# Four transformer layers on one core: the rotation reads queries and keys from the projection's bank, and two orders are changed in the attention slots

## The reference

```python
q = (x @ Wq).reshape(B, S, H, hd).transpose(0, 2, 1, 3)   # 32 heads of 16
k = (x @ Wk).reshape(B, S, G, hd).transpose(0, 2, 1, 3)   # 8 groups
v = (x @ Wv).reshape(B, S, G, hd).transpose(0, 2, 1, 3)
q = _apply_rope(q, cos, sin)          # t * cos + rotated * sin
k = _apply_rope(k, cos, sin)
scores = jnp.einsum('bhqd,bhkd->bhqk', q, k)               # keys repeated 4 times
scores = jnp.where(causal[None, None], -jnp.inf, scores)
attn = jax.nn.softmax(scores / jnp.sqrt(jnp.float32(hd)), axis=-1)
ctx = jnp.einsum('bhqk,bhkd->bqhd', attn, v).reshape(B, S, D)
return ctx @ Wo
```

## Time and profile before

| | |
|---|---|
| median of 3 runs | 1228.06 us (1227.69 to 1230.71) |
| the profiled execution's own time | 1229.5 us |
| its span | 1227.8 us |
| busy: TensorE matmul | 1149.5 us (94%) |
| busy: VectorE | 782.8 us (64%) |
| busy: ScalarE | 655.9 us (53%) |
| busy: GpSimd | 506.8 us (41%) |
| mean granted TensorE clock | 0.989 |
| slots of run 0 end | about 545 us |
| slots of run 1 begin | about 835 us |

### The profile page before, as it was taken

How to read it: one execution, slowest core, us unless ns; L and a number is a source line. 1 busy time by engine, 2 the same in 40 slices (tenths; PEclk the granted TensorE clock), 3 DMA queues, 4 the chain that set the end, 5 groups by cost and what they waited for, 6 DMA issues and landing times.

```text
span 1227.8 us, 22076 instructions
## 1 busy us (share of the span) xinstructions
PE 1149.5 (94%) x8476; PEld 845.0 (69%) x8476; DVE 782.8 (64%) x1124; ACT 655.9 (53%) x1199; POOL 506.8 (41%) x648
## 2 busy tenths in 40 slices
PE   5999999999999999989999999999999999899997
PEld 4788877766656656556687788777666667676565
DVE  7843458786875646674644465545777887875545
ACT  4433348675565555554323333326866666766654
POOL 0000127565422112124555454512965566655552
PEclk9999989999999999999999999998999999999999
DMA  7000010030000100010242222211000100000001
GB/s 275 1 1 1 1 36 3 2 114 2 2 2 2 39 1 2 27 53 27 79 153 85 96 77 81 94 42 50 6 2 2 43 2 20 19 17 34 2 1 69
DMA packets 15258, 48.04 MB, mean 39 GB/s; under 512 B 2858, under 2 KB 6959, under 8 KB 14388
## 3 DMA queue, kind: packets, MB, share of 16 engines
q1 hardware_dynamic: 15156, 46.63, 11.3%
HBM read 44.00 MB, written 2.10 MB: 38 GB/s over the span
## 4 chain that ended last, share of the span: by engine, by line
PE 67%; DVE 18%; ACT 6%; issue 5%; DMA 2%; POOL 2%; DVEq 0%; ACTq 0%; SPq 0%; POOLq 0%
PE bank L679 18%; PE bank L812 13%; PE bank L712 9%; PE bank L950 8%; DVE negmax L1906 6%; PE bank L925 5%; PE bank L863 3%; PE bank L905 3%; ACT probs L1446 2%; DMA W_lo_whole<-in_w 2%; DVE rope_sin L1893 1%; PE bank L829 1%; DVE W_lo_whole L1676 1%; PE bank L872 1%; DVE pvT L1934 1%
## 5 line engine op out<-in xcount | busy, mean ns | idle before, releaser
L1906 DVE TENSOR_REDUCE negmax<-bank 128x4 f32<-128x1024 f32 (+1 forms) x256 | 250.0, 1016 | 75.7 <-PE bank L872 56.6
L1446 ACT ACTIVATE probs<-bank 128x512 f32<-128x512 f32 (+1 forms) x224 | 188.2, 846 | 48.0 <-PE bank L905 46.8
L2139 POOL TENSOR_SCALAR_AFFINE_SELECT probs<-probs 128x512 f32<-128x512 f32 x192 | 128.3, 678 | 136.7 <-ACT probs L1446 135.8
L2061 POOL TENSOR_TENSOR W_lo<-W_lo_whole,W_hi 128x512 fp32r<-128x512 f32 x84 | 117.2, 1424 | 100.6 <-ACT W_hi L1175 100.6
L925 PE MATMUL bank<-probs,V 128*32 128x256 f32 (+1 forms) x2048 | 117.7, 348 | 6.7 <-DVE negmax L1906 3.5
L863 PE MATMUL bank<-kT,qT 64*128 64x256 f32 (+1 forms) x1024 | 102.1, 295 | 10.5 <-DVE xT_lo L1557 5.5
L1175 ACT ACTIVATE W_hi<-W_lo_whole 128x1536 fp32r<-128x1536 f32 x28 | 41.7, 1489 | 131.4 <-DVE W_lo_whole L1676 131.4
L1457 ACT ACTIVATE pv<-bank 128x256 f32<-128x256 f32 x128 | 49.7, 388 | 109.2 <-PE bank L925 97.4
L905 PE MATMUL bank<-qT,kT 64*128 64x256 f32 (+1 forms) x512 | 97.4, 396 | 11.0 <-ACT qT L1418 3.3
L2108 POOL TENSOR_TENSOR scaled<-pvT,recip 128x256 f32<-128x256 f32 x64 | 41.9, 654 | 146.5 <-DVE recip L1937 146.2
L925 PEld LDWEIGHTS bank<-probs,V 128*32 128x32 f32 x2048 | 54.0, 110 | 62.2 <-issue 28.9
(11 more groups left out here) (214 smaller groups left out, 2687.2 us busy)
## 6 DMA issues: line engine op xcount, KB each, us to landing
W_lo_whole<-in_w SPq DMA_DIRECT2D x28, 768.0 KB, 4.2
Wqkv_lo_whole<-in_Wqkv SPq DMA_DIRECT2D x6, 768.0 KB, 7.0
Wo_lo_whole<-in_Wo SPq DMA_DIRECT2D x4, 1024.0 KB, 4.9
Wqkv<-in_Wqkv SPq DMA_DIRECT2D x2, 1536.0 KB, 7.2
Wdown_whole<-in_Wd SPq DMA_DIRECT2D x1, 2816.0 KB, 14.8
x<-in_x SPq DMA_DIRECT2D x4, 512.0 KB, 6.2
out<-x SPq DMA_DIRECT2D x8, 256.0 KB, 2.0
V_lo_whole<-in_V SPq DMA_DIRECT2D x1, 1408.0 KB, 6.1
```

What stands on the lines that cost most here:

```text
L1446: nc.scalar.activation(A[l].probs[gi % 2][kb][:, :, q0 - kb * A[l].probs1:].rearrange("p (b h) q -> p b h q", b=2), B.tensor(key)[:, :, 0: ...
L1906: v.tensor_reduce(A[l].negmax[u % 2][:, qb, :].rearrange("p (b h) -> p b h", b=2)[:, :, 2 * g:2 * g + 2], B.tensor(key)[:, :, 0:2 * nk].re ...
L2061: ins = gp.tensor_tensor(lo, whole, hi.bitcast(F32), ALU.subtract)
L2139: gp.affine_select(out=blk, in_=blk, compare_op=ALU.is_ge, fill=0.0, base=0, pattern=[[0, 4], [1, P]], channel_multiplier=-1).then_inc(cau ...
```

## The change

For the projections that are taken inside the slots (units 3 to 7 of layers 0 and 2, all units of layer 3) ScalarE copies only V from the bank (`take_values`), with a semaphore of its own (`values_taken`). VectorE waits for it and multiplies by cosine and sine straight from the bank (`rope_direct`); the second multiplication frees the bank, and an addition closes the rotation. It stands in the odd slot of the projection itself, behind the transposes of values and context and ahead of the tile's low part and the residual. Projections ahead of the slots (`FROM_COPY` = 6 of layers 0 and 2) keep the old way. TensorE runs the first row scores ahead of the first column scores in even slots, in both runs and all four layers. GpSimd runs the context's low part, then the stack's, ahead of the scaling.

```diff
+FROM_COPY = 6
...
-        rope_part = mark("rope_parts", [32, 0, 32, 32])
+        rope_part = mark("rope_parts", [22, 0, 22, 16])
+        v_taken = mark("values_taken", [10, 0, 10, 16])
...
+                if g % 2 == 0 and G + LEAD < RUN * GROUPS:
+                    scores_rows(r, G + LEAD, 0)
                 scores_cols(l, u, g, 1)
                 if G + LEAD < RUN * GROUPS:
-                    scores_rows(r, G + LEAD, 0)
+                    if g % 2 == 1:
+                        scores_rows(r, G + LEAD, 0)
                     scores_rows(r, G + LEAD, 1)
...
+            def take_values(l, u, tau):
+                key = ("qkv", l, u, tau)
+                act.wait_ge(*B.filled(key))
+                nc.scalar.activation(A[l].V[u % 4][:, tau, 0:4, 0:HD], B.tensor(key)[:, 320:384].rearrange("p (h d) -> p h d", d=HD),
+                                     copy).then_inc(v_taken.sem, 1)
...
-                if g % 2 == 1 and U + 3 < RUN:
+                if g % 2 == 1 and U + 3 < RUN and ROPE[unit(r, U + 3)[0]]:
+                    take_values(*unit(r, U + 3), g // 2)
+                if g % 2 == 1 and U + 3 < RUN and not ROPE[unit(r, U + 3)[0]]:
                     take_projection(*unit(r, U + 3), g // 2)
...
+            def rope_direct(l, u, tau):
+                i = 2 * u + tau
+                key = ("qkv", l, u, tau)
+                first = values_before(l)
+                dve.wait_ge(*v_taken.at(l, i + 1 - first))
...
+                src = B.tensor(key)[:, 0:320].rearrange("p (h d) -> p h d", d=HD)
+                tc, ts = A[l].rc[i % 2], A[l].rs[i % 2]
+                halves = [P, 20, 2, HD // 2]
+                v.tensor_tensor(tc[:], src, cosT[l][:, tau, :].unsqueeze(1).to_broadcast([P, 20, HD]),
+                                ALU.mult).then_inc(rope_part.sem, 1)
+                v.tensor_tensor(ts[:].rearrange("p h (e d) -> p h e d", e=2),
+                                src.rearrange("p h (e d) -> p h e d", e=2)[:, :, ::-1, :],
+                                sinT[l][:, tau, :].rearrange("p (e d) -> p e d", e=2).unsqueeze(1).to_broadcast(halves),
+                                ALU.mult).then_inc(B.empties(key), 1)
+                dve.wait_ge(*rope_part.at(l, first + i + 1))
+                dve.wait_ge(*B.emptied(key))
+                v.tensor_tensor(A[l].qkr[i % 2][:], tc[:], ts[:], ALU.add).then_inc(rope_done.sem, 1)
...
+                if G == 0:
+                    rope(*unit(r, 2), 1)
+                if g % 2 == 1 and U + 3 < RUN and ROPE[unit(r, U + 3)[0]]:
+                    rope_direct(*unit(r, U + 3), g // 2)
                 if r == 1 and tile_turned(U, g) is not None:
                     transposed_low(3, tile_turned(U, g))
...
-                if g == 0 and U + 2 < RUN and ROPE[unit(r, U + 2)[0]]:
-                    rope(*unit(r, U + 2), 1)
-                if g == 3 - U % 2 and U + 3 < RUN and ROPE[unit(r, U + 3)[0]]:
-                    rope(*unit(r, U + 3), 0)
...
-                if pair_complete(G) is not None:
-                    scale_context(r, pair_complete(G))
+                if pair_turned(G - 1) is not None:
+                    context_low(r, pair_turned(G - 1))
...
                 if g < 2 and U + 2 < RUN:
                     stack_low(*unit(r, U + 2), g)
+                if pair_complete(G) is not None:
+                    scale_context(r, pair_complete(G))
...
-                if pair_turned(G - 1) is not None:
-                    context_low(r, pair_turned(G - 1))
```

More of the change, by code:

```diff
@@ L604, in pair, with values_before @@
             return 2 * r + q // n, q % n
+        def values_before(l):
+            return FROM_COPY if l % 2 == 0 else 0
         block = ctx.enter_context(nc.Block())
@@ L1378, in take_projection @@
                 if before and ROPE[before[0]]:
-                    act.wait_ge(*rope_part.at(before[0], 2 * (2 * before[1] + tau + 1)))
+                    act.wait_ge(*rope_part.at(before[0], min(2 * (2 * before[1] + tau + 1), 2 * FROM_COPY)))
                 elif before:
@@ L1898, in rope @@
                 v.tensor_tensor(A[l].qkr[i % 2][:], tc[:], ts[:], ALU.add).then_inc(rope_done.sem, 1)
+            def rope_direct(l, u, tau):
[3 more added lines that the diff above has]
+                dve.wait_ge(*v_taken.at(l, i + 1 - first))
+                if earlier(l, u):
+                    ll, n = earlier(l, u)[0], 2 * earlier(l, u)[1] + tau + 1
+                    if ROPE[ll]:
+                        dve.wait_ge(*rope_done.at(ll, n))
+                    dve.wait_ge(*stack_hi.at(ll, HI * n))
+                    dve.wait_ge(*stack_lo.at(ll, 2 * n))
+                src = B.tensor(key)[:, 0:320].rearrange("p (h d) -> p h d", d=HD)
[10 more added lines that the diff above has]
+                v.tensor_tensor(A[l].qkr[i % 2][:], tc[:], ts[:], ALU.add).then_inc(rope_done.sem, 1)
             def row_max(r, G, qb):
```

## The result

The changed kernel takes 1238.66 us in the median of 4 runs (1237.06 to 1239.97), beside 1228.60 (1227.69 to 1230.71) for the kernel before on the same chip: 1.0079 times as long, with an interval of 1.0059 to 1.0098. The direction was forecast and the range held it; the size was not: +10 us instead of +4.5.

What follows compares the result with a forecast made beforehand. TensorE was taken as the bound, waiting most for VectorE. Costs of 3.75, 2.1, 0.25, 1.4 and 0.8 less gains of 1.3, 0.4, 0.35, 0.5 and 1.2 gave +4.55 us: 1232.5 us forecast, 1217 to 1240 eight times in 10.

Steps and rivals of the forecast that it cites:

- Part 1, the bank: Projections inside slots: VectorE frees the bank later, so second row scores start 0.25 us later in 15 slots, +3.75 us.
- The 65 ns: Rotation's multiplications: extra VectorE access time for a bank, making the wait 0.38 instead of 0.25 us, 2 us more.
- Part 2, VectorE: VectorE's work behind the rotation delays output projections by 0.35 us in six slots, +2.1 us.
- the upper case: Unit 5, group 1: rotation's addition ends at 946.6 instead of about 946.25 if GpSimd's low part overlaps it.
- Part 3, tiles: Run 1's eight slots with tile transposes: rows wait for the tile's low part behind the rotation, +1.4 and +0.8 us.
- Part 4, gains: GpSimd's context low part first: -1.3, -0.4, -0.35 us; rows first: -0.5 in run 1, -1.2 in layer 1.
- the 0.4: Layer 0, same place as unit 2 to 3 of run 1: output projection earlier through context's low part, -0.4 us.
- Layer 0's tile slot: Layer 0's slot with a tile: gain from the context's low part going ahead of other GpSimd work, -0.35 us.
- The step that failed is layer 1: Layer 1: rows first starts the maxima 0.35 us earlier, which counts in three or four slots, -1.2 us.
- The second rival: Slots: TensorE's wait for the last exponential before the values may absorb the 0.25 us, leaving 1229 us; chance 0.20.
- VectorE's relief wins: Layers 2 and 3: all 11.4 us of stalls from VectorE's and GpSimd's lateness go, giving 1219 us; chance 0.24.

Runs made afterwards that it cites:

- GpSimd's order alone: Kernel before, with only GpSimd's low parts (context's, then stack's) moved ahead of the scaling: 1220.33 us, 0.9944.
- rows first alone: Kernel before, with only the first row scores of even slots moved ahead of the first column scores: 1229.39 us, 1.0014.
- the copied rotation: Kernel before with both new orders and the rotation in its new place, but still reading ScalarE's copy instead of the bank: 1251.68 us, 1.0202.
- the rotation alone: Changed kernel with TensorE's and GpSimd's orders put back, leaving only the rotation from the bank in its new place: 1239.00 us, 1.0095.
- rotation and GpSimd's order: Changed kernel with row scores again behind the first column scores in even slots: 1240.67 us, 1.0100.
- GpSimd's old order in the changed kernel: Changed kernel with GpSimd's scaling put back ahead of the low parts: 1241.42 us, 1.0102.
- the moved statistics: Changed kernel with the row statistics of group 1 moved to group 2, ahead of the residual: 1233.93 us, 1.0050.
- the last of the three order kernels: Kernel before, with the context's low part moved on GpSimd ahead of the inverse deviation but left behind the scaling: 1226.70 us, 0.9993.

## Why the prediction was right or wrong

**Part 1, the bank (3.75 us).** The mechanism, the duration (0.49) and the wait (0.24 of 0.25) were right, from a bound taken between 0.447 and 0.69. What reaches the end was not. Nine of the pairs counted lengthen by 0.23, 0.17, 0.15, 0.27 (units 0 to 2 of run 0; the last has an output projection behind it), 0.22, 0.13, 0.01, 0.26 and 0.15 (run 1, units 0 to 2, 11 and 12), 1.6 us in all, a mean of 0.18. So a part is taken up later; by which wait was not followed. Those of group 3 of odd units, counted at 0.05, show -0.01 to 0.06 in run 1. The 65 ns that the Trainium skill has for a bank (Perfetto Trace Analysis, "Optimizing Scalar/DVE Operations") were not found in full: the first multiplication takes 0.491 us, 44 ns above its fastest from SBUF (0.447), and the second 0.480, 8 ns above its own (0.472). The rule of the Trainium skill on two inputs in SBUF (SBUF — State Buffer, "Who interferes with whom") agreed for the multiplications: 490 to 492 ns from the bank, 447 to 1762 from SBUF. As the prediction words it ("only if two of its inputs are in SBUF") it is too narrow: `vareps` reads one tile alone and took 0.68 us beside GpSimd's low part, 0.17 otherwise.

**Part 2, VectorE (2.1 us).** Right in place and cause, undersized: six output projections cost 0.49, 0.47, 0.43, 0.45, 0.46 and 0.60, 2.9 us. The stretched addition was named as the upper case (946.6 instead of 946.25) and is what happened, because the change itself moved GpSimd's scaling beside it.

**Part 3, tiles (1.4 + 0.8 us).** Group 3: +0.64, +0.67, +0.03, +0.19, 1.5 us, as forecast. Group 1 of run 1: +0.27, +0.19, -0.08, +0.08, 0.5 us.

**Part 4, gains.** The pair of unit 2, group 3 gained 1.18, close to the forecast with the 0.25 of part 1 in it; the same place in layer 0 gained nothing (10.73 to 11.00; 10.72 with GpSimd's order alone): the 0.4 was a false analogy. Layer 0's tile slot gained 0.70 (forecast 0.35). **The step that failed is layer 1**: "VectorE had waited 0.35 us for the rows, and they would come by that much earlier". They do, and nobody waits for them; what comes later is what TensorE waits for. Layer 1 in the kernel before, behind the values at 416.85:

```profile
418.44 1.09 ACT L1441 ACTIVATE probs<-bank 128x512 f32<-128x512 f32 x2
...
418.63 2.36 DVE L1906 TENSOR_REDUCE negmax<-bank 128x4 f32<-128x1024 f32 x2 [3.45 <-PE bank L863]
...
419.18 1.00 PE L829 MATMUL bank<-ident_r,qstack 128*128 128x128 f32 x8
```

and with rows first alone, behind the values at 415.35:

```profile
416.89 2.35 DVE L1909 TENSOR_REDUCE negmax<-bank 128x4 f32<-128x1024 f32 x2 [3.21 <-PE bank L863]
...
417.18 1.09 ACT L1444 ACTIVATE probs<-bank 128x512 f32<-128x512 f32 x2 [0.31 <-PE bank L895]
...
417.92 1.00 PE L829 MATMUL bank<-ident_r,qstack 128*128 128x128 f32 x8 [0.36 <-ACT probs L1444]
```

The maxima start 0.24 us earlier after the values (1.54, before 1.78), the exponentials 0.24 later (1.83, before 1.59), and the query transposes wait for these: 2.57 instead of 2.33. Ten slots of layer 1 lose 0.11 to 0.31 each, 2.3 us, and one gains 0.5; in that one the clock is at half for part of the time in both kernels, and not for the same part. Pairs of kernels with and without rows first agree: 303.39 against 301.61, 302.94 against 301.00, and 304.37 against 301.55, this one with a clock drop in a slot. So +1.8 or 1.9 (+1.3 in the changed kernel beside the one before) instead of -1.2. The second rival named that wait for the exponential in the rotated layers; I didn't look for it in layer 1, which has no rotation.

**The rest of the profiles' 7.5 us.** Forecast 4.55; layer 1 adds 2.5 (+1.33 instead of -1.2), the slots of the rotated layers take off 0.6, and the other stretches add 1.0; the very end alone adds 1.1, where the last matmuls run at half clock (PEclk is the sixth value):

```profile
1220.00:1225.00 5.00, 5.00 (x16) 2.42 (x14) 2.39 (x5) 1.18 (x3) 0.00 (x0) 0.87 0.01 2
1225.00:1230.00 5.00, 5.00 (x13) 3.81 (x12) 3.03 (x5) 1.97 (x4) 0.00 (x0) 0.50 0.05 20
```

In the kernel before and in eleven of the twelve others this end, from the last values on, takes 56.65 to 56.80 us, here 57.79, and 57.99 with the copied rotation, whose last matmuls ran at half clock too. The -1.07 ahead of the slots and the +0.92 between the runs lie within what kernels with the same work there differ by (178.46 to 180.73 and 262.62 to 267.39).

**The medians' 10 us.** The profiled execution of before lies 0.9 above 1228.60, and the one of after 1.6 below its median, so the medians' difference is 2.5 larger than the profiles'. Part of that goes with the clock. Within each kernel, over 120 executions in all, 0.001 of mean granted clock goes with 0.45 us, and with half of the variance. Brought to the mean clock 0.990 by that slope, an estimate, before has 1228.5 and after 1237.3 us, 8.8 apart; rows first alone 1229.2, GpSimd's order alone 1221.4, the rotation alone 1238.9, rotation and GpSimd's order 1240.6, the copied rotation 1246.2.

**The sum of the parts.** By medians the rotation costs 11.3 us beside the old orders, of which run 1's first 13 units show 7.6 and layer 0 3.1. Rows first earns its 1.8 us of layer 1 back by covering the bank: without rows first the units 0 to 12 take 270.80, with it 266.72. GpSimd's order is worth 7.3 us beside the old rotation, and beside the new one it gives nothing that can be told (1240.67 with it, 1239.00 without). It took most of its gain from an old rotation stretched by GpSimd, and the moved one is no longer there. So the rival "VectorE's relief wins" was half right: such stalls could be had, 7 us of them, but one moved line of GpSimd gets them, and moving the rotation spends more than they are worth.

**Open.** What makes the clock fall in some kernels' slots (the copied rotation, GpSimd's old order in the changed kernel, once the moved statistics) and not in others; a wait of 1.09 us for GpSimd stands ahead of one fall, and a wait of 1.12 in the kernel before has none behind it. A kernel with rows first, GpSimd's order and the old rotation was not run. Beside the copied rotation it would give the price of the new place directly; as it stands, that price is read from single places (4.18 to 4.59 and 5.08 us).

## What to carry to other kernels

An instruction whose inputs are ready must not stand behind one that waits for another engine: one line moved ahead of such a wait gave 7 us, the same line moved up but left behind the wait gave nothing that can be told, and the whole change cost 10. When an order is swapped, follow both sides to the engine that is the bound, the work that comes later as well as that which comes earlier, and in every stage that the loop serves. Before a difference of pairs is put down to an order, look at the durations of the matmuls there.

## What the runs showed of the hardware that was not expected

The granted clock fell to half for about 3.4 us at a time also in the middle of slots in which TensorE is busy nine tenths of the time. In units 0 to 12 of run 1 that happened four times in two of the fourteen profiled executions, once in a third, and not once in the eleven others (1.7 us each, an estimate). The mean clock goes with half of the spread of one and the same kernel: the kernel before had 1223.96 us at 0.996 and 1234.01 at 0.985. VectorE's small instructions are stretched like the large ones: the one on 128x2 elements at 954.75, beside the context's low part of the last of the three order kernels, took 0.68 us, and 0.17 where GpSimd was idle. One that reads a bank and one tile is not: 490 to 492 ns over all 36.
